# Preparing the next token group's layer norm inside the feed-forward part's first matmul

## The reference

```python
def layernorm(x, eps=1e-5):
    return (x - mean(x)) / sqrt(var(x) + eps)      # over the last axis

x = x + attn(layernorm(x), W_qkv, W_out)           # x: 8 x 2048 x 1024 fp32, 16 heads, causal
h = relu(layernorm(x) @ w1 + b1)                   # w1: 1024 x 4096
x = x + h @ w2 + b2                                # w2: 4096 x 1024
```

## Time and profile before

| | |
|---|---|
| median of three runs | 1304.41 us |
| the profiled execution's own time | 1312.34 us |
| its span, slowest core (core 5) | 1310.8 us |
| spans of the eight cores | 1295.7 to 1310.8 us |
| TensorE matmul busy | 985.3 us, 75% |
| VectorE busy | 472.6 us, 36% |
| ScalarE busy | 411.8 us, 31% |
| chain that ended last | TensorE 64%, DMA 15%, VectorE 13% |

### The profile page before, as it was taken

The page is one execution under the profiler, slowest core; times in us unless marked ns, Lnnn a source line. Parts: engine busy times, 40 slices in busy tenths (PEclk is TensorE's granted clock), DMA queues, the critical chain, the costliest instruction groups (busy, mean ns, idle before and its releaser), DMA issues.

```text
span 1310.8 us, 12768 instructions; the slowest of 8 cores (1295.7 to 1310.8 us)
## 1 busy us (share of the span) xinstructions
PE 985.3 (75%) x4656; PEld 391.6 (30%) x4656; DVE 472.6 (36%) x638; ACT 411.8 (31%) x443; POOL 80.1 (6%) x107
## 2 busy tenths in 40 slices
PE   1279889585858677695958176796999789988997
PEld 0134322121213222221312032343344334443443
DVE  0542242645454444636351722311341134212401
ACT  0124167475756666574759100001000100010000
POOL 2100200000000000000000001021002100110010
PEclk9989888696979889796968598898899889988998
DMA  8920711000000002000020089999439953894476
GB/s 192 182 13 1 63 17 17 1 9 8 9 8 1 1 0 33 1 1 1 1 32 1 0 191 154 167 149 206 128 96 137 179 162 100 130 169 154 126 119 139
DMA packets 102653, 101.59 MB, mean 77 GB/s; under 512 B 40128, under 2 KB 81088, under 8 KB 102592
## 3 DMA queue, kind: packets, MB, share of 16 engines
q0 software_dynamic: 60288, 50.41, 29.2%
q10 hardware_dynamic: 33280, 33.56, 8.2%
q1 hardware_dynamic: 9024, 16.80, 4.2%
HBM read 134.37 MB, written 16.78 MB: 115 GB/s over the span
## 4 chain that ended last, share of the span: by engine, by line
PE 64%; DMA 15%; DVE 13%; ACT 3%; issue 3%; DVEq 2%; POOL 0%; ACTq 0%; POOLq 0%
PE arena L762 17%; PE arena L716 13%; PE arena L518 11%; PE arena L375 9%; PE arena L463 6%; DMA wstage<-w1b 5%; DVE tmp_sb L627 5%; PE arena L297 5%; DVE oscr_sb L534 3%; DMA wstage<-w 3%; DVE x_sb L638 3%; DMA wstage<-wqkv 3%; DMA wstage<-wout 2%; PE arena L478 2%; DVEq L54 1%
## 5 line engine op out<-in xcount | busy, mean ns | idle before, releaser
L491 ACT ACTIVATE p_sb<-arena,cst_sb 128x1024 bf16<-128x1024 f32 (+1 forms) x320 | 291.1, 987 | 98.8 <-PE arena L463 61.9
L518 PE MATMUL arena<-p_sb,vaug_h 128*128 128x512 bf16 (+3 forms) x640 | 193.5, 388 | 142.1 <-DVE oscr_sb L534 94.2
L716 PE MATMUL arena<-lnf_sb,wstage 128*128 128x512 bf16 x1024 | 239.5, 398 | 60.8 <-DMA wstage<-w1b 35.1
L762 PE MATMUL arena<-w2stage,h_sb 128*128 128x512 bf16 x1024 | 221.7, 379 | 4.0 <-DVE h_sb L730 4.0
L730 DVE TENSOR_SCALAR h_sb<-arena,b1c_sb 128x512 bf16<-128x512 f32 x128 | 96.1, 750 | 214.2 <-PE arena L716 214.2
L716 PEld LDWEIGHTS arena<-lnf_sb,wstage 128*128 128x128 bf16 x1024 | 102.8, 102 | 196.4 <-issue 89.1
L762 PEld LDWEIGHTS arena<-w2stage,h_sb 128*128 128x128 bf16 x1024 | 99.9, 98 | 125.8 <-issue 5.9
L375 PE MATMUL arena<-lnf_sb,wstage 128*128 128x512 bf16 x512 | 126.3, 404 | 6.3 <-DMA wstage<-wqkv 6.3
L463 PE MATMUL arena<-qpair,kpair 64*128 64x512 bf16 (+3 forms) x640 | 126.2, 390 | 4.9 <-DVE kpair L398 4.9
L518 PEld LDWEIGHTS arena<-p_sb,vaug_h 128*128 128x128 bf16 x640 | 42.7, 100 | 205.5 <-issue 204.1
L391 DVE CAST qpair<-arena 64x512 bf16<-64x512 f32 x64 | 43.7, 683 | 147.8 <-PE arena L375 147.1
(11 more groups left out here) (37 smaller groups left out, 442.0 us busy)
## 6 DMA issues: line engine op xcount, KB each, us to landing
w2stage<-w POOLq DMA_DIRECT2D x64, 512.0 KB, 7.0
wstage<-w1b ACTq DMA_DIRECT2D x24, 1024.0 KB, 7.1
x_sb<-x SPq DMA_DIRECT2D x4, 2048.0 KB, 14.4
wstage<-w POOLq DMA_DIRECT2D x8, 1024.0 KB, 12.7
w1b<-wstage ACTq DMA_DIRECT2D x8, 1024.0 KB, 8.7
y<-y_sb SPq DMA_DIRECT2D x16, 512.0 KB, 9.2
wstage<-wqkv POOLq DMA_DIRECT2D x24, 256.0 KB, 11.7
wstage<-wout POOLq DMA_DIRECT2D x4, 512.0 KB, 18.7
```

What stands on the lines that cost most here:

```text
L491: e.activation(AP(p_sb, (si_ % 3) * 1024, [[3 * 1024, 128], [512, 2], [1, w_]]), AP(arena, b_ + off_, [[AR, 128], [512, 2], [1, w_]]), AF. ...
L518: e.matmul(AP(arena, (4 + hx) * 512 + off_, [[AR, 128], [1, w_]]), vaug_h[:, hx, j_ * 128:(j_ + 1) * 128], AP(p_sb, (si_ % 3) * 1024 + hx ...
L716: (lambda s_, dc_, fb_, wp_: lambda e: e.matmul(bankap(fb_, TF), AP(wstage, s_ * 1024 + dc_ * 512 + wp_ * 128, [[8 * 1024, 128], [1, 128]] ...
L762: (lambda s_, ww_, c2_, dh_, t_: lambda e: e.matmul(bankap(t_, 512), h1_sb[:, ww_, 128 * c2_:128 * (c2_ + 1)], w2stage[:, s_, 512 * dh_:51 ...
```

## The change

The layer norm of group g + 1 moves from FFN2 of group g, and from the head of group g + 1, into FFN1 of group g. Statistics of tiles 0 and 1 are listed ahead of step 2, those of tiles 2 and 3 and the square root and reciprocal ahead of step 4. Apply and transpose of tiles 0 to 3 are listed ahead of steps 6, 10, 14 and 18. The transposes now go through banks 6 and 7, which FFN1 does not use, and the result goes to another 512 columns of `lnf_sb` than the ones being read (`lpar`). Only group 0 keeps its layer norm at its head. FFN2's matmul on bank 6 waits for the last evacuation of the transposes.

```diff
         def ln_transpose(dst_sb, dst_tok0, parity, vv_app, extra_tp=(),
-                         buf=None, np_=4, free_tbl=None):
+                         buf=None, np_=4, free_tbl=None, bank67=False):
...
+            base = 6 * 512 if bank67 else (2 * (pb % 2)) * 512
+            bfree = ln67_state["free"] if bank67 else ln_bank_free[pb % 2]
...
-            for t in range(4):
-                c = g * 4 + t
-                extra_tp = ([("ex", ex_attn_done)] if (g == 0 and t <= 1)
-                            else ([ffn2_evac4] if (g > 0 and t <= 1) else []))
-                ln_transpose(lnf_sb, t * 128, t, ln2_apps[g % 2][t],
-                             extra_tp=extra_tp)
+                for t in range(4):
+                    extra_tp = [("ex", ex_attn_done)] if t <= 1 else []
+                    ln_transpose(lnf_sb, lpar + t * 128, t,
+                                 ln2_apps[g % 2][t], extra_tp=extra_tp)
             vv_ln2 = lnf_state["ready"]
+            ob67 = ([out_bank_free[6], out_bank_free[7]]
+                    if out_bank_free else [("ex", ex_attn_done)])
             for ww in range(NWW):
+                if g + 1 < NG:
+                    if ww == 2:
+                        vst = ln_stats((g + 1) * 4 + 0, ((g + 1) % 2) * 4)
+                        vst = ln_stats((g + 1) * 4 + 1, ((g + 1) % 2) * 4 + 1)
+                    elif ww == 4:
+                        vst = ln_stats((g + 1) * 4 + 2, ((g + 1) % 2) * 4 + 2)
+                        vst = ln_stats((g + 1) * 4 + 3, ((g + 1) % 2) * 4 + 3)
+                        ln2_rstd[(g + 1) % 2] = ln_rstd(((g + 1) % 2) * 4,
+                                                        4, vst)
+                    elif ww in (6, 10, 14, 18):
+                        t = (ww - 6) // 4
+                        app = ln_apply_only((g + 1) * 4 + t,
+                                            ((g + 1) % 2) * 4 + t, t,
+                                            ln2_rstd[(g + 1) % 2])
+                        ln_transpose(lnf_sb, ((g + 1) % 2) * 512 + t * 128,
+                                     t, app,
+                                     extra_tp=(ob67 if t == 0 else ()),
+                                     bank67=True)
                 if ww % 4 == 0:
...
-                                    lnf_sb[:, dc_, 0:TF],
+                                    lnf_sb[:, dc_, lp_:lp_ + TF],
...
+                    elif t == 6 and ww == 0 and ln67_g is not None:
+                        w0 = [ln67_g]
...
-            if g + 1 < NG:
-                vst = 0
-                for t in range(4):
-                    vst = ln_stats((g + 1) * 4 + t, ((g + 1) % 2) * 4 + t)
-                ln2_rstd[(g + 1) % 2] = ln_rstd(((g + 1) % 2) * 4, 4, vst)
-                ln2_apps[(g + 1) % 2] = [
-                    ln_apply_only((g + 1) * 4 + t, ((g + 1) % 2) * 4 + t,
-                                  t, ln2_rstd[(g + 1) % 2],
-)
-                    for t in range(4)]
```

More of the change, by code:

```diff
@@ L237, in ln_apply_only @@
                 waits=[("vv", vv_rstd)], inc="vv")
+        ln67_state = {"free": None}
         def ln_transpose(dst_sb, dst_tok0, parity, vv_app, extra_tp=(),
-                         buf=None, np_=4, free_tbl=None):
+                         buf=None, np_=4, free_tbl=None, bank67=False):
             buf = lntm_sb if buf is None else buf
@@ L253, in ln_transpose @@
                     identb[:, :], start=True, stop=True,
-                    skip_group_check=True))(pb, dc, buf),
+                    skip_group_check=True))(pb, dc, buf, base),
                     waits=w0, inc="tp" if dc == DC - 1 else None)
             free_tbl[pb] = ("tp", tp_last)
-            ex_ev = add("scalar", (lambda t0, p_, d_: lambda e: e.activation(
+            ex_ev = add("scalar", (lambda t0, d_, ba_: lambda e: e.activation(
                 d_[:, :, t0:t0 + 128],
-                AP(arena, (2 * (p_ % 2)) * 512,
-                   [[AR, 128], [128, 8], [1, 128]]),
+                AP(arena, ba_, [[AR, 128], [128, 8], [1, 128]]),
                 AF.Identity))(
-                dst_tok0, pb, dst_sb),
+                dst_tok0, dst_sb, base),
                 waits=[("tp", tp_last)], inc="ex")
-            ln_bank_free[pb % 2] = ("ex", ex_ev)
+            if bank67:
+                ln67_state["free"] = ("ex", ex_ev)
+            else:
+                ln_bank_free[pb % 2] = ("ex", ex_ev)
             lnf_state["ready"] = ("ex", ex_ev)
@@ L715, in build_program @@
                     mm_f1 = add("tensor",
-                                (lambda s_, dc_, fb_, wp_: lambda e: e.matmul(
+                                (lambda s_, dc_, fb_, wp_, lp_: lambda e:
+                                 e.matmul(
                                     bankap(fb_, TF),
@@ L737, in build_program @@
             vv_h1 = C["vv"]
+            ln67_g = ln67_state["free"] if g + 1 < NG else None
             for ww in range(NWW):
```

12 lines of the change are left out of this document (7 added, 5 removed).

## The result

The changed kernel takes 1339.9 us (median of eight runs, 1335.6 to 1340.8); the kernel before took 1304.95 us (eight runs, 1303.6 to 1307.5). The ratio is 1.0261 with a 95% interval of 1.0247 to 1.0274: 35 us slower. The forecast was 1348 us, range 1320 to 1372, slower. Its profiled execution took 1337.8 us, its slowest core (core 7) spanning 1336.3 us.

What follows compares the result with a forecast made beforehand. FFN2 was at TensorE's rate, group 0's FFN1 load-bound, borders held by loads behind ScalarE's evacuations. Groups 1, 2, 3 and 0 gave 28.3 + 29.9 - 17.2 + 3 = +44.0 us on 1304.41: 1348 us, range 1320 to 1372.

Steps and rivals of the forecast that it cites:

- The borders: Three gaps between FFN2 and the next FFN1: evacuation wait, transposes and load wait go, leaving about 0.1 us.
- Step 4 of group 1: In FFN1, its load waits behind the square root and lands in 7.39 us; start at +20.8 us, 13.9 idle.
- The cycle: FFN1 of groups 1 and 2, loads for steps 8 to 20 held behind transposes: 15.0 us instead of 6.9.
- Rival B: Milder cycle in FFN1: the clock may stay at 2.4 GHz and loads land in 5.3 us; 1324 us, chance 0.13.
- Groups 1 and 2: Border and FFN1 together, slowed by held loads and waits for the apply: +28.3 and +29.9 us.
- Group 3: Border and FFN1 together: prepares nothing, one wait at step 8; 58.0 against 75.2 us, so -17.2.
- Group 0: FFN1: transposes of step 18 delay the rest, others hide under load waits; +3 us, bounds 0 and +8.
- FFN2: One more 1 MB load beside the w2 loads, landing in 6 to 7 us: costs nothing, at worst 2 us a group.
- The sum: All groups' terms together: +44.0 us, giving 1348 us on the median of the runs.
- D: ScalarE's sequencer runs past waiting activations, so each load goes out when its buffer is free; 1272 us, chance 0.04.
- C: Harder cycle: loads land in 7.4 us, starts lose 3.1, group 0's late store reaches its chain; 1371 us, chance 0.11.
- E: No change in time: borders gained and cycles lost cancel, which needs each load hidden again; chance 0.02.

Runs made afterwards that it cites:

- e6: The changed kernel with its list in the same order, bf16 weight loads issued through GpSimd's stream instead of ScalarE's; 1307.4 us, ratio 0.9977.
- e7: The changed kernel with, in group 0 only, statistics at steps 4, 6, 8, 10 and transposes at 14, 18, 22, 26; 1342.3 us, ratio 1.0206.
- e1: The changed kernel with step 4's load (group 0: store) listed ahead of the statistics of tiles 2 and 3 and the square root; 1322.3 us, ratio 1.0113.
- e8: The changed kernel with group 0's stores of the bf16 weights issued from SyncE instead of ScalarE; 1342.2 us, ratio 1.0225.
- e4: The kernel before, layer norm where it was, with bf16 weight loads listed one tile earlier; 1284.4 us, ratio 0.9815.
- e2: As e1, with every load of the bf16 weights also listed one tile (four steps) earlier; 1305.7 us, ratio 0.9985.
- e3: As e2, with statistics at steps 4, 6, 8, 10 and each apply one step ahead of its transposes; 1273.4 us, ratio 0.9743.
- e9: As e3, with both first loads of group 1 issued in the middle of group 0's FFN2, behind a matmul wait; 1282.9 us, ratio 0.9739.
- e3_again: Repetition of e3, unchanged, made beside the last series of runs; 1273.7 us, ratio 0.9718.

## Why the prediction was right, step by step

The forecast's kind, sign and mechanism held; most terms were somewhat large. For group 1, us from its start (906.19 on core 7) or lengths:

```
step                                   forecast   measured
second load issued                       +13.2      +13.0
its landing                               7.39       5.22
step 4 starts                            +20.8      +18.5
steps 4 and 5 (3.46 at full clock)        6.16       5.14
wait for the apply                        1.85       1.99 to 2.03
eight transposes                          1.02       0.61
one cycle                                15.0       13.45
  of it issue, landing, start             6.4        5.5
  of it clock loss                        2.3        1.7
step 20 starts                           +81.3      +72.6
FFN1's last matmul ends                 +104.4      +93.5
```

**The borders.** Forecast 0.1 us, measured -0.1 (the modelled end of the last matmul overlaps the next): right.

**Step 4 of group 1.** The issue came within 0.2 us of the forecast, so the count of VectorE's work up to the square root was right. The landing was mis-sized: I took the one row on the chain, 7.39, but after's landed in 5.22, with no other load or store beside it. In the chain of the kernel after (start, us, what):

```profile
919.21 5.22 DMA wstage<-w1b
```

All five loads that TensorE waited for in this group landed in 5.2 to 5.3 us, the low end of the earlier trace rows, and not in its median. The Trainium skill, DMA: Bandwidth & Descriptors, gives a fit for transfers of GpSimd's path, 2.0 us and bytes by 436 GB/s; an estimate by it is 4.4 us for 1 MiB. No run here shows that: e6's 24 such loads took 5.8 us at the least and 6.2 in the median.

**The cycle.** 13.45 against 15.0: the landing 0.8, the clock loss 0.6, the transposes 0.4 lower, the apply wait 0.2 higher. The loss is the difference between 5.30 and 3.62 us for the same sixteen matmuls at 937.93 and 932.24. Rival B had it that 2 us of idle time costs no clock. On core 7 it does in group 1. In group 2 some starts behind a load wait are at the full rate, but the loss is then behind the transposes:

```profile
1096.50 0.61 PE L253 MATMUL arena<-identb_sb,lntm_sb 128*128 128x128 bf16 x8 [2.03 <-DVE lntm_sb L233]
1096.94 3.62 PE L742 MATMUL arena<-lnf_sb,wstage 128*128 128x512 bf16 x16
1102.62 3.61 PE L742 MATMUL arena<-lnf_sb,wstage 128*128 128x512 bf16 x16 [2.06 <-DMA wstage<-w1b]
...
1108.70 5.30 PE L742 MATMUL arena<-lnf_sb,wstage 128*128 128x512 bf16 x16
...
1128.88 22.57 PE L742 MATMUL arena<-lnf_sb,wstage 128*128 128x512 bf16 x96 [4.03 <-DMA wstage<-w1b]
```

Taken over 3.61 us for sixteen, the stretches of 5.93, 5.11, 5.30 and 22.57 us (the last of ninety-six) lost 7.3 us in group 2, and those of group 1 lost 8.0 (5.14, three of 5.30, 4.90 and 20.88), so B had the loss wrong in both. What differs is where it falls: the sixteen matmuls behind a transpose run while the load is still out, and a slow stretch there shortens the wait that follows (0.53 us behind sixteen matmuls of 5.11 us at 1085.22, against 2.06 behind the full-rate ones at 1096.94). So one cycle there is 11.8 us (1096.50 to 1108.26). The last load of the group, 7.2 us long, and the low clock behind it bring the group to 94.3 all the same. B was right in the landing and wrong in the clock. By the medians the truth (+35) is nearer to the forecast (+44) than to B (+20), by the stages of the two traces (+27) nearer to B.

**Groups 1 and 2** were forecast at +28.3 and +29.9 and measured (mean of cores) +17.6 and +18.8: eleven us each too large, which is the table above.

**Group 3** was forecast at -17.2, measured -15.8. Its one wait came where it was expected, but took longer beside the y stores, a landing of 9.89 us:

```profile
1216.79 9.89 DMA wstage<-w1b
```

**Group 0** was forecast at +3 by the transposes of step 18, with the others hidden under load waits. FFN1 measured +5.0, and here the step itself failed, not a size. The four waits for the apply (5.03, 2.03, 2.03, 2.03) were put at nothing but the last, and are not hidden: e7, which leaves about 1 us of them and moves the statistics as well, brings FFN1 8.9 us down, and FFN1 with FFN2 7.1. I had costed the first at 1.85 behind an arrival of TensorE that is later than the statistics; step 6 comes first there. And the chain that ended last ran through the store of tile 1, which I had excluded:

```profile
768.09 9.02 DMA w1b<-wstage
777.64 11.83 DMA wstage<-w
789.53 10.56 DMA w1b<-wstage
800.63 10.91 DMA wstage<-w
811.61 9.81 DMA w1b<-wstage
822.11 17.12 DMA wstage<-w
```

That store was issued at 768.09, as forecast (768.2). But a place on the chain is not a cause: e1 and e8 took the delay away, and FFN1 of group 0 kept 91.0 and 89.0 us. Loads and stores alternate on this chain in either case. Read with e7, what sets it is when TensorE frees the buffers; no run shows that by itself.

**FFN2** was costed at nothing. For groups 1 to 3 that holds to 0.1 us; for group 0 it was 1.3, within the 2 us given as the worst. That one load took 17.2 us to land on core 7, not the 6 to 7 of the forecast, and cost nothing there only because it was needed late. It was nearly the right number for the changed kernel and the wrong habit for the next ones: with both loads ahead of w2's, this stage takes 4 to 6 us more, on cores without the odd clock.

**The sum.** +44.0 forecast, +35 by the medians, +27 by the stages in the mean of the cores. The last is the measure of the terms, which were worked out from the same trace of before: they were 17 us too large, 21.8 of it in groups 1 and 2, the other way in group 0 with FFN2 (+6.3 for +3) and in group 3. That the measured time lies 8 us from the forecast, and not 17, comes from which executions were traced, and is luck. Group 0's FFN1 lies between 83.2 and 97.1 us from core to core after, between 81.8 and 90.0 before. How that spread comes about was not tried.

**The rivals.** D, loads that go out when their buffers are free, is refuted by the issue times for this kernel, whose waits are instructions of their own, and by e6, which shows what D would have looked like in its loads. C is refuted by the landings of 5.2 us and by group 0 at 93.5 us, under its mark of 98. E needed each load hidden; none was. Of the marks set beforehand: the load at 13 us into the group came; the idle time by w1b was 41.0 us in 11 pieces, 37.7 of it in groups 1 and 2 (51 in 10 or 11); twelve apply waits came, 27.3 us (22); FFN1 of groups 1 and 2 missed its mark of 100 us by five to six; group 3 had 60.4 for 58.

## What to carry to other kernels

On an engine that computes and issues DMAs, list each load ahead of every operation that waits for something later than the load's own buffer, or issue it from an engine without such waits; here that was worth 1.9% in the kernel before (e4) and 2.7% in the changed one (e2). Moving work from a border into a loop lost time here until each piece was listed a step later than its input: the waits for the same applies came to 27 us with transposes at steps 6 to 18 and to 3 us with the apply a step ahead of them. A load brought forward can land on other traffic: here two of them, ahead of the w2 loads, took back 4 to 6 us in one stage. When a stage looks bound by a load, compare the issue time with the time that its buffer came free before trusting the transfer's length.

## What the runs showed that was not expected

The granted clock had a value apart from its two levels in group 0, on one pair of neighbouring cores in four of the executions (e1 cores 4 and 5, e2 cores 4 and 5, e3 cores 2 and 3, e9 cores 0 and 1). In e9, cores 0 and 2 in the same 50 us:

```profile
core 0: us, PE busy (x) PEld busy (x) DVE busy (x) ACT busy (x) POOL busy (x), PEclk, DMA share, GB/s
850.00:900.00 50.00, 48.73 (x184) 20.14 (x186) 0.00 (x0) 0.00 (x0) 8.24 (x12) 0.81 0.82 142
```

```profile
core 2: us, PE busy (x) PEld busy (x) DVE busy (x) ACT busy (x) POOL busy (x), PEclk, DMA share, GB/s
850.00:900.00 50.00, 46.48 (x213) 20.31 (x212) 0.78 (x2) 0.00 (x0) 9.79 (x14) 1.00 1.03 176
```

At 0.81 the 256 matmuls of FFN2 take 69.6 to 70.7 us instead of the 59.5 to 66.6 of the other cores in these executions, and the slowest core sets the time: e9's profiled execution spans 1284.1 us on core 0 and 1251.0 on core 3. The value was there from 754 to 774 us, the start of FFN1 of group 0, until 916 to 935, with stretches at half clock between. In e3 and e9 it began at 754 to 760 us. The first load that these two list otherwise than e7 stands at step 28, some 70 us later, and e3_again is the same program as e3; neither e7 nor e3_again showed the value. So in these two the moved loads did not bring it on. What does is open, and four of twelve executions are few.

Smaller ones: in quiet stretches a 1 MB load lands in 5.2 us from ScalarE's queue and in 5.8 to 6.3 from GpSimd's; beside the y stores one took 9.9. GpSimd is held for 0.88 us by each issue, ScalarE's queue for 0.37.
